# A decoder layer with routed experts: second normalisation, scatters and expert results put in another order

## The reference

```python
# after x = _layernorm(x + self_attention(x))
x = _layernorm(x + _L0_xattn_ref(x, ctx_1024, ctx_1024, mask, ...))

logits = einsum('bsd,de->bse', x, Wg) + bg
topk_vals, topk_idx = top_k(logits, 2)
topk_w = softmax(topk_vals)
h = relu(einsum('bsd,edf->bsef', x, W1) + b1)
eo = einsum('bsef,efd->bsed', h, W2) + b2
sel = take_along_axis(eo, topk_idx[..., None], axis=2)
y = sum(sel * topk_w[..., None], axis=2) + x
x = gamma * (y - mean(y)) * rsqrt(var(y) + eps) + beta
x = _layernorm(x)
```

## Time and profile before

| | us |
|---|---|
| median of 3 runs | 916.0 (915.48 to 917.31) |
| the profiled execution | 919.0 |
| its span, first to last instruction | 917.2 |
| TensorE busy | 767.4 (84%) |
| VectorE busy | 618.7 (67%) |
| ScalarE busy | 459.7 (50%) |
| GpSimd busy | 306.5 (33%) |

### The profile page before, as it was taken

One profiled execution on the slowest core, in us unless ns is written; L12 is line 12 of the kernel. 1 busy time (PEld: TensorE's weight loads), 2 busy tenths in 40 slices (PEclk: granted clock), 3 DMA queues, 4 the chain that ended last, 5 costly groups with the idle time before them and its releaser, 6 DMA issues.

```text
span 917.2 us, 14858 instructions
## 1 busy us (share of the span) xinstructions
PE 767.4 (84%) x4736; PEld 380.5 (41%) x4736; DVE 618.7 (67%) x981; ACT 459.7 (50%) x920; POOL 306.5 (33%) x315
## 2 busy tenths in 40 slices
PE   6789999999999999999888868891899999999400
PEld 3442222222222222222235545561587777777300
DVE  3588888887888878888548975866165333357446
ACT  2126777777777777777764231431344444445100
POOL 8001400000002979600126552535502210244674
PEclk9889999999999999999999976995799999999755
DMA  6746030302205897900007100001222322332221
GB/s 192 185 86 149 3 86 18 87 18 56 50 19 144 259 279 249 281 13 1 0 1 314 53 1 0 1 1 40 95 70 97 105 89 82 98 89 70 82 85 46
DMA packets 52146, 82.44 MB, mean 90 GB/s; under 512 B 15913, under 2 KB 40745, under 8 KB 50921
## 3 DMA queue, kind: packets, MB, share of 16 engines
q1 hardware_dynamic: 40009, 48.27, 18.9%
q0 software_dynamic: 9280, 31.20, 10.3%
q10 hardware_dynamic: 2784, 2.02, 1.1%
HBM read 48.15 MB, written 33.03 MB: 89 GB/s over the span
## 4 chain that ended last, share of the span: by engine, by line
PE 62%; DVE 18%; POOL 7%; DMA 4%; issue 4%; ACT 3%; SPq 1%; POOLq 0%; DVEq 0%; ACTq 0%
PE bank L514 11%; PE bank L506 11%; PE quad L487 10%; PE quad L818 9%; PE bank L832 6%; DVE rowmax L894 6%; PE bank L615 3%; PE bank L438 2%; POOL yg L1652 2%; ACT probs L1336 2%; PE quad L586 2%; DVE max L1002 1%; DVE sc L997 1%; DVE xres L971 1%; PE bank L623 1%
## 5 line engine op out<-in xcount | busy, mean ns | idle before, releaser
L894 DVE TENSOR_REDUCE rowmax<-quad 128x1 f32<-128x1024 f32 x256 | 303.0, 1219 | 74.4 <-PE quad L487 73.8
L1336 ACT ACTIVATE probs<-bank 128x512 f32<-128x512 f32 x512 | 283.9, 595 | 111.7 <-PE bank L506 109.1
L506 PE MATMUL bank<-qstack,kstack 98*128 98x512 bf16 x512 | 193.4, 386 | 12.3 <-ACT probs L1336 10.2
L487 PE MATMUL quad<-kstack,qstack 96*128 96x512 bf16 x512 | 177.8, 387 | 13.0 <-DMA qstack<-q_parts 6.7
L514 PE MATMUL bank<-probs,v_all 128*32 128x512 f32 x1024 | 138.1, 608 | 0.0
L506 PEld LDWEIGHTS bank<-qstack,kstack 98*128 98x128 bf16 x512 | 48.9, 97 | 190.8 <-ACT probs L1336 162.5
L818 PE MATMUL quad<-xbT,w_all 128*128 128x128 bf16 x1104 | 99.6, 224 | 8.6 <-issue 5.1
L818 PEld LDWEIGHTS quad<-xbT,w_all 128*128 x1104 | 76.3, 97 | 33.2 <-issue 17.1
L487 PEld LDWEIGHTS quad<-kstack,qstack 96*128 96x128 bf16 x512 | 48.5, 99 | 74.4 <-DVE rowmax L894 37.6
L1447 ACT ACTIVATE xbT<-bank 128x512 bf16<-128x512 bf16 x46 | 27.4, 598 | 98.1 <-PE bank L799 98.1
L832 PE MATMUL bank<-w_all,hh 128*128 x368 | 68.7, 275 | 8.4 <-DVE hl L1098 8.1
(11 more groups left out here) (176 smaller groups left out, 964.2 us busy)
## 6 DMA issues: line engine op xcount, KB each, us to landing
w_all<-w_split SPq DMA_DIRECT2D x2, 4096.0 KB, 18.0
xb<-x_sorted SPq DMA_DIRECT2D x46, 128.0 KB, 2.3
y_sorted<-ysb SPq DMA_DIRECT2D x46, 128.0 KB, 1.7
x_sorted<-zeros POOLq DMA_DIRECT2D x6, 768.0 KB, 6.9
w1raw<-in_w POOLq DMA_DIRECT2D x8, 512.0 KB, 5.3
w2raw<-in_w POOLq DMA_DIRECT2D x8, 512.0 KB, 5.7
w_split<-w1two POOLq DMA_DIRECT2D x8, 512.0 KB, 4.3
w_split<-w2two POOLq DMA_DIRECT2D x8, 512.0 KB, 3.2
```

The lines of the kernel that those rows point to most:

```text
L487: mm = pe.matmul(bank[2 * (p % 2) + e], q, kstack[slot][0:MAXROW, j, e * 512:e * 512 + 512], start=True, stop=True)
L506: mm = pe.matmul(bank[4 + i % 2], kstack[slot][0:KROWS, j, kt * P:kt * P + P], qstack[slot][0:KROWS, half, j, :], start=True, stop=True)
L894: dve.tensor_reduce(rowmax[:, k % 2, p:p + 1], quad[:, 2 * (p % 2):2 * (p % 2) + 2, :].rearrange("p a n -> p (a n)"), AX_X, ALU.max).then_ ...
L1336: act.activation(probs[:, i % PR, :], bank[4 + i % 2], ACT.Exp, scale=INV4).then_inc(probs_ready, 1)
```

## The change

It has two parts, both in one kernel.

*The cross-attention.* On VectorE the moments, the root and the normalisation of group g follow its residual directly, ahead of the next `take`; `turn_x2` and `keep_x2` stand one tile earlier. Four of the last eight tiles get their self-attention residual before the tile loop begins, and the other four in its first and third tile. The routing logits go with tiles 9 and 13 (`SCORED`). `place(0)` stands at the end of tile 11, and the ranks between the two halves of the value matmuls of group 2. The scatters of the first half stand at tile 11 (4), 12 (4) and 13 (8).

*The results.* A sorted row now is 258 float32 words: the 256 that held the high and low halves, twice the token's number, and its first expert. From these and the block's expert VectorE computes for each row of a block the number of the row where its result belongs (`send_rows`): 2 x token for the first choice, one more for the second. Padding rows carry 2048 and fall out by the bounds check. GpSimd sends each finished block there with one indirect DMA (`send_block`), so `y_tokens` has the results of a token side by side, and SP and ScalarE load them with four plain DMAs of 512 KB for a half (`load_outputs`). The gathers and SP's stores of blocks are gone. The moments of the last two norms are computed on VectorE with one power on GpSimd, and statistics and norms stand at separate blocks (`MIX`, `FIRST`, `LAST`). x2 + beta goes to buffers of its own (`xbeta`, in the space of `kbd` and `vbd`), at blocks 20 to 26.

```diff
-XB, YB = 8, 3
+XB, YB = 8, 6
+XW = D + 2
...
-        NORM2 = (5, 8, 12)
+        SCORED = (9, 13)
         BLOCKS = 2 * HB
-        MIX, FIRST, LAST, SHOWN = (HB + 10, HB + 18), (HB + 14, HB + 21), (HB + 18, HB + 22), (HB + 20, None)
-        SPREAD1, SPREAD0 = [5 + 7 * j // 8 for j in range(2 * HT)], [HB + 1 + j for j in range(2 * HT)]
+        MIX, FIRST, LAST = (HB + 6, HB + 12), (HB + 9, HB + 15), (HB + 12, HB + 18)
+        FETCHED = HB + 9
+        SPREAD1 = [5 + j // 2 if j < HT else 1 + j for j in range(2 * HT)]
...
+        def await_outputs(eng, h):
+            for i in range(YB):
+                eng.wait_ge(ys_stored[i], 16 * len(range(i, (h + 1) * HB, YB)))
+
+        def load_outputs(eng, h, i):
+            src = ys[h][4 * P * i:4 * P * (i + 1), :].rearrange("(n p j) d -> p n (j d)", n=2, j=2)
+            eng.dma_start(yg[:, 2 * i:2 * i + 2, :, :].rearrange("p n j d -> p n (j d)"), src).then_inc(yg_loaded[i], 16)
...
-                if i == 2 and g:
+                if i == 1 and g:
                     turn_x2(g - 1)
...
+            def send_rows(m):
+
+                h, i, r = m // HB, m % HB, m % XB
+                dve.wait_ge(xb_loaded[r], 16 * (m // XB) + 16)
+                dve.scalar_tensor_tensor(dest[:, r:r + 1], xtag[:, r, 1:2], table[:, h, i:i + 1], xtag[:, r, 0:1],
+                                         ALU.not_equal, ALU.add).then_inc(dest_done, 1)
...
                 if i == 0 and g:
                     bn = residual2(g - 1)
+                    link(bn)
+                    start_moments(4 * g - 4, 4 * g)
+                    root_moments(4 * g - 4, 4 * g)
+                    norm_x2(g - 1)
                 if n + FAR < NT:
                     take(n + FAR)
...
-                if n - 1 in NORM2:
-                    j = NORM2.index(n - 1)
-                    root_moments(4 * j, 4 * j + 4)
-                    norm_x2(j)
-                if n in NORM2:
-                    j = NORM2.index(n)
-                    link(bn)
-                    start_moments(4 * j, 4 * j + 4)
...
+            def send_block(m):
+
+                h = m // HB
+                pool.wait_ge(y_done, m + 1)
+                pool.indirect_dma_start(ys[h], bass.IndirectOffsetOnAxis(ap=dest[:, m % XB:m % XB + 1], axis=0), ysb[:, m % YB, :], None, bounds_check=2 * S - 1, oob_is_err=False).then_inc(ys_stored[m % YB], 16)
...
-            scatter(range(HT, NT), SPREAD1)
-            gather(0, range(0, 6))
...
+            for m in range(BLOCKS):
+                send_block(m)
+                for j, at in enumerate(SPREAD1):
+                    if at == m:
+                        pool.wait_ge(h_ready, m + 4)
+                        scatter(HT + j // 2, j % 2)
+                if m in (HB - 3, HB - 1, HB + 1, HB + 3):
+                    add_beta((m - (HB - 3)) // 2)
```

More of the change, by code:

```diff
@@ L617, in values2 @@
                     mm.then_inc(o2_ready, 1)
+                    if ranked and half == 0:
+                        pe.wait_ge(s2_taken, NT - 1)
+                        rank(0)
+                        rank(1)
             def project_o2(g):
@@ L782, in _ @@
                 if i == 3:
[L783 removed]
+                    values2(g, n == NT - 5)
                     project_o2(g)
[L785 to L788 removed]
             def turn_block(m):
@@ L1483, in _ @@
                         finish_tiles(g)
+            await_outputs(act, 1)
+            act.wait_ge(mixed, 2)
+            for i in range(1, HT // 2, 2):
+                load_outputs(act, 1, i)
             finish_tiles(2)
@@ L1627, in _ @@
                         divide(n + m)
+                if n == 2:
+                    root(2, KT, NT)
+                if i == 0 and g:
+                    root(2 + g, 4 * g - 4, 4 * g)
+                if n == NT - 4:
+                    for i in range(2, 4):
+                        for j in range(2):
+                            scatter(i, j)
                 if n + FAR < NT:
                     shift(n + FAR)
-                if n == 3:
-                    root(2, KT, NT)
-                if n in NORM2:
-                    j = NORM2.index(n)
-                    root(3 + j, 4 * j, 4 * j + 4)
@@ L1654, in add_beta @@
-            def add_beta(g):
-                pool.wait_ge(mixed, g + 1)
-                pool.tensor_tensor(xres[:, 4 * g:4 * g + 4, :], xres[:, 4 * g:4 * g + 4, :],
+                if i < 2 and 4 * (g + 1) < NT:
+                    add_bias2(4 * g + 4 + 2 * i)
+                    add_bias2(4 * g + 5 + 2 * i)
+                if n == NT - 5:
+                    for i in range(0, 2):
+                        for j in range(2):
+                            scatter(i, j)
+                elif n == NT - 3:
+                    for i in range(4, HT):
+                        for j in range(2):
+                            scatter(i, j)
@@ L1698, in _ @@
-            for k, g in MOMENTS:
-                if (k, g) == (1, 0):
-                    gather(0, range(6, HT))
-                if (k, g) == (0, 2):
-                    gather(1, range(HT))
-                if (k, g) == (1, TG - 2):
-                    root(7, NT - 4, NT)
-                    add_beta(3)
-                moments(k, g)
-                if k == 0:
-                    add_beta(g)
-            root(8, NT - 4, NT)
+            for m in range(BLOCKS):
[6 more added lines that the diff above has]
+                    add_beta((m - (HB - 3)) // 2)
+                for g in range(2):
+                    for k, at in enumerate((MIX, FIRST)):
+                        if m == at[g] + 1:
+                            root(7 + ORDER.index((k, g)), 4 * g, 4 * g + 4)
@@ L1712 @@
+            for k, g in ORDER[4:]:
+                root(7 + ORDER.index((k, g)), 4 * g, 4 * g + 4)
 def kernel(**inputs):
```

238 lines of the change are left out of this document (106 added, 132 removed).

## The result

The changed kernel takes 884.3 us (882.6 to 888.0, four runs) against 916.65 us (915.5 to 918.6) of the kernel before in the same comparison: a ratio of 0.965 (95% interval 0.962 to 0.969). 32 us are gained, not 48, and the time lies 0.3 us above the top of the predicted range. The profiled execution took 888.0 (span 886.2), where the sum gave 870.7: 17.3 us are to be explained.

What follows compares the result with a forecast made beforehand. TensorE waits on GpSimd's divisions and VectorE's normalisation in the cross-attention, paces the expert loop, and is done before the tail. Gains 15.6 + 0 + 12.2 + 9.2 + 11.3 = 48.3 give 870.7 profiled, median 867.7; range 857 to 884.

Steps and rivals of the forecast that it cites:

- Step 1: Cross-attention: second normalisation ahead of the next take shortens the first value-block interval, 15.6 us gained; second interval unchanged.
- measured clean group: Cross-attention before the change: middle interval between value blocks, without either long wait, 39.1 us, reused for the first interval.
- The 1.2 for the moments ahead of a take: Cross-attention start: the last eight tiles' moments in front of one take put the first value block 1.2 us later.
- Step 2: Cross-attention, third interval: smaller scatter lots cut TensorE's 16.9 us wait on a division to about 8.2, 12.2 us gained.
- Step 3: End of expert loop: moments on VectorE and earlier sums with beta remove the waits on hl, 9.2 us gained.
- Step 4: Expert loop: 46 indirect sends by block, 1.26 us each on GpSimd, replace plain stores and gathers without slowing blocks.
- Rival (c): Expert loop: GpSimd becomes the bound if a checked send takes over 5.1 us; at 5.4, 929 us; chance 0.03.
- Step 5: Tail: last kept block to the end takes 40.2 us against 51.5, 11.3 us gained.
- rival (b): Tail: the output loads share the engines, making the first mix 5.4 us later, 873 us; chance 0.10.
- (a): Cross-attention: normalisation before the take costs what it saves, three groups each 5 us longer, 883 us; chance 0.19.
- (d): Cross-attention and expert loop: long wait returns at another tile (12.2 lost), hl still late (9.2 lost), 889 us; chance 0.05.
- (e): Cross-attention: TensorE's slow-clock stretches go with the waits, 3 us in each of three groups, 859 us; chance 0.08.

Runs made afterwards that it cites:

- gap_filled: Changed kernel with the eight transposes of x2 issued three times over, only to keep TensorE busy: 876.5 us, ratio 0.956.
- logits_later: Changed kernel with the first group's logits back in front of the scores of tile 10 instead of tile 9: 881.5 us, ratio 0.962.
- take_first: Changed kernel with the last pair's residual, statistics and start of moments behind the take and maximum of tile 5 instead of ahead: 883.2 us, ratio 0.962.
- filled_full: Changed kernel with early logits reading, later biases and last-pair residual, x2 transposes issued 4, 4, 5 times, ranks inside the value block's second half, two store queues: 872.3 us.
- bias_later: Changed kernel with GpSimd's first two sums with the bias of each group behind the two divisions instead of ahead: 881.4 us, ratio 0.964.
- the repeat: The changed kernel itself measured once more, nothing edited: 885.7 us, ratio 0.965.
- results_only: Changed kernel with the cross-attention's old order restored, results still sent by block: 899.4 us, ratio 0.982.
- norm_behind: Changed kernel with moments, root and second normalisation behind the next tile's take, and four scatters moved behind the shift: 896.1 us, ratio 0.975.
- lots_of_eight: Changed kernel with the first eight scatters in one lot again, behind the shift of tile 15: 889.5 us, ratio 0.971.
- best: filled_full with the ranks again between the value block's halves and the low half of tiles 4 to 7 split three tiles later: 871.7 us, ratio 0.952.

## Why the prediction was right or wrong

**Step 1, the length of the first two intervals: wrong, and it is the step that failed.** "I take the measured clean group, 39.1, for the first interval", and 0 for the second. They measured 45.1 and 44.7, and these are 11.6 of the 17.3 us. The 8.9 us wait did go (2.1 is the longest on the normalisation now, 1.1 VectorE's wait on a root).

What I missed first is the clock. I took over a group of 39.1 with a stretch at 0.83 in it as though the clock belonged to the work. The same matmuls at 0.85 instead of 0.95 over the interval are 4.2 of the 5.7 us of the second. That it is the clock which costs is shown by gap_filled (more work, a higher clock in all four runs, 8 us less time) and, in one execution each, by logits_later (36.8 with the clock up, 44.9 with it down) and take_first (40.1 where nothing was edited). In take_first the forecast 39.1 is nearly met, so how much of the miss is clock differs from execution to execution; both executions of the changed kernel itself had 44.7 or more.

What I missed second is in the same diff: SCORED moves the logits from tiles 10 and 14 to 9 and 13. Before, a value block lay between the logits of tile 10 and the next scores and hid VectorE's reading of them; now only 1.2 us of transposes lie between a tile's scores and the next ones, and TensorE waits 2.2 and 2.3 us. I costed the moved normalisation and not this moved step. The clean group had waits too (2.1 on a division and 1.7 on the normalisation), so the idle time grew by only 1.4. The narrow logits also stand right behind the wait on the division now. Whether it is this place or the longer idle time that lengthens the low stretch stays open: with the logits moved away (logits_later) and with the idle time filled (filled_full) the clock held, and each is one execution.

The biases in pairs, now ahead of the division, add 1.4 us to the wait on it, of which 1.0 would fall to the take behind it otherwise (bias_later). I had them at nothing.

**The start of that step: half right.** The 1.2 for the moments ahead of a take was 3.2 in the profiled execution and 0.9 in the repeat. The mechanism is confirmed: with this chain behind the take the wait is 0.7 and the stretch 21.2 us (take_first). The wait itself was 4.1 and 2.5 in two executions of one kernel; why isn't shown.

**Step 2, smaller lots: right in mechanism, and lucky in the last digit.** 36.8 was forecast and 36.76 measured, but the two waits are 6.4 and 0.7 where I had 8.2 and 1.0, so something else took 2.1 us more than I allowed. Undoing the lots alone brought a wait of 16.8 us back. (The divisions behind the eight scatters of before are those of tiles 14 and 15; the prediction says 13 and 14, and its sum doesn't depend on it.)

**Step 3, the end of the expert loop: right in mechanism.** No wait on hl above 0.6 us, and the last kept block 7.55 us behind the last hidden block started, where I had 7.1. The gain was 7.1 and not 9.2: 1.3 us went because the pace is 4.115 us per block between blocks 8 and 36, not 4.07, for which I had left 0 to 4 blocks by 1.3 as bound, and 0.4 at the last block. TensorE's waits there name no engine ("issue"), so I don't give it a cause. The results_only kernel gained 8.1 in this stretch.

**Step 4, the sends: right.** 1.06 us with the check, 1.36 with 0.3 of idle behind it, where I took 1.26. Rival (c), the one that ends slower, needed 5.1.

The rows of 1032 bytes, for which the prediction names 0.6 us and leaves them out of its sum, cost nothing that shows: the first hidden block starts 12.1 us behind the last value block, 12.2 before.

**Step 5, the tail: right.** 39.55 against 40.2. The two pairs of loads didn't share to the end: first mix E+7.5 against E+8.2, so rival (b) is out as well.

**The rivals.** (a) gave the right number, 883, for the wrong reason: its groups, 5 us longer each, are what happened in two of three, but with the order that it blames undone (norm_behind) the time is 10 us longer and not shorter. (d) and (c) didn't occur. (e) had the mechanism that was in play, the slow-clock stretches, with the wrong sign: I asked what would come if they went, never what if they grew. A stretch grown by 6 us in each of two groups stands 12 above the forecast, at 880, before any other miss; with (a) weighed beside it the range would have gone past 884.

## What to carry to other kernels

A "clean" stretch borrowed from the trace is only clean for the order of instructions and the clock that it had: look at its granted clock and list every consumer whose cover lies in it before its length is reused. When a diff moves a step, check for each moved one what lay between the producer and the next user; here a value block had hidden VectorE's reading. And where TensorE shows waits of a few us with half clock behind them, giving it useless work in the gap is a cheap test of whether the clock or the chain is the cost.

## What the runs showed of the hardware

The granted clock isn't a function of the waits alone. In seven groups (two of the changed kernel, two of its repeat, two of lots_of_eight, the second of logits_later) a wait of 2.9 us on the division was followed by 0.61 or 0.62 over 17 us. In an eighth, the second of take_first, the order and the waits are the same (2.9 and 2.3 us), and the clock was 0.86 over 12.4 us. Shorter waits were followed by low stretches too: 1.5 us (bias_later), 1.2 us (gap_filled) and 0.7 us (best, first group), while behind 1.0 us at the same place in filled_full it held. What decides in a given execution I can't say. It makes single traces of this kernel differ by several us at one and the same program, so that a gain read from one trace has to be held against the times.

Duplicate transposes in an idle gap gained 8 us here, though they are extra work. Four of the eight last stores on another queue gained nothing: E to the end stayed at 39.6 us.

A VectorE instruction on 128x4 values took 2.10 us when it fell into a GpSimd subtraction and 0.17 us when it didn't (norm_behind against the changed kernel).
